# A graph network in one kernel: one row tile in five of the attention weights is transposed by a DMA on 16-bit halves instead of by TensorE

## What is computed

```python
def _sparse_attention(x, src, dst, wq, bq, wk, bk, wv, bv, wo, bo):
    q = (x @ wq + bq).reshape(N, H, Dh) * Dh ** (-0.5)
    k = (x @ wk + bk).reshape(N, H, Dh)
    v = (x @ wv + bv).reshape(N, H, Dh)
    scores = jnp.einsum('ehd,ehd->eh', q[src], k[dst])
    ex = jnp.exp(scores - smax[src])
    attn = ex / denom[src]
    out = jax.ops.segment_sum(attn[:, :, None] * v[dst], src, num_segments=N)
    return out.reshape(N, D) @ wo + bo
```

## Time and profile before

| | |
|---|---|
| time, median of 3 runs | 1119.53 us (1119.40 to 1120.54) |
| span of the profiled execution | 1117.2 us (its time outside the profile isn't recorded) |
| PE busy | 1066.1 us, 95% of the span |
| DVE busy | 773.4 us, 69% |
| ACT busy | 577.6 us, 52% |
| POOL busy | 673.3 us, 60% |
| granted TensorE clock, mean | 0.992 of full speed |
| one turn of the middle loop | 141.1 us |

### The profile page before, as it was taken

One profiled execution on the slowest core, in us unless ns is written; L12 is line 12 of the kernel. 1 busy time (PEld: TensorE's weight loads), 2 busy tenths in 40 slices (PEclk: granted clock), 3 DMA queues, 4 the chain that ended last, 5 costly groups with the idle time before them and its releaser, 6 DMA issues.

```text
span 1117.2 us, 20722 instructions
## 1 busy us (share of the span) xinstructions
PE 1066.1 (95%) x6808; PEld 987.7 (88%) x6808; DVE 773.4 (69%) x1535; ACT 577.6 (52%) x1032; POOL 673.3 (60%) x923
## 2 busy tenths in 40 slices
...
DMA packets 40963, 56.92 MB, mean 51 GB/s; under 512 B 14312, under 2 KB 14812, under 8 KB 40735
## 3 DMA queue, kind: packets, MB, share of 16 engines
...
q10 hardware_dynamic: 260, 0.21, 0.1%
...
## 4 chain that ended last, share of the span: by engine, by line
PE 79%; DVE 6%; POOL 5%; ACT 4%; issue 3%; DMA 2%; DVEq 0%; POOLq 0%; SPq 0%; PEldq 0%; ACTq 0%
PE ps L340 42%; PE ps L1768 8%; PE ps L362 8%; PE ps L786 5%; PE ps L2101 3%; PE ps L2028 3%; PE ps L2402 3%; POOL w_lo L380 2%; ACT away L737 1%; PE ps L2065 1%; PE ps L1259 1%; PE ps L1246 1%; PE ps L1742 1%; DMA w_raw<-L_gnn_wk 1%; PE ps L1220 1%
## 5 line engine op out<-in xcount | busy, mean ns | idle before, releaser
L380 POOL TENSOR_TENSOR w_lo<-w_raw,w_hi 128x512 fp32r<-128x512 f32 x152 | 204.8, 1348 | 12.7
L340 PE MATMUL ps<-yt_hi,w_hi 128*128 128x314 f32 (+2 forms) x640 | 201.8, 315 | 2.8 <-DVE yt_lo L2236 1.6
L340 PE MATMUL ps<-yt_hi,w_lo 128*128 128x314 f32 (+2 forms) x640 | 197.6, 309 | 0.0
L340 PE MATMUL ps<-yt_lo,w_hi 128*128 128x314 f32 (+2 forms) x640 | 197.3, 308 | 0.0
L459 POOL TENSOR_SCALAR prob<-prob,rinv 125x628 f32<-125x628 f32 x160 | 126.4, 792 | 105.2 <-DVE rinv L444 86.9
L403 ACT ACTIVATE pt_hi<-ps 125x625 fp32r<-125x625 f32 x160 | 109.2, 694 | 102.9 <-PE ps L362 101.7
L377 POOL TENSOR_SCALAR w_hi<-w_raw 128x512 fp32r<-128x512 f32 x152 | 97.7, 643 | 95.3 <-DMA w_raw<-L_gnn_wo 28.8
L340 PEld LDWEIGHTS ps<-yt_hi,w_hi 128*128 128x128 f32 x640 | 121.8, 190 | 5.9 <-issue 4.4
L340 PEld LDWEIGHTS ps<-yt_hi,w_lo 128*128 128x128 f32 x640 | 121.7, 190 | 0.0
L340 PEld LDWEIGHTS ps<-yt_lo,w_hi 128*128 128x128 f32 x640 | 121.5, 190 | 0.1
L786 PE MATMUL ps<-oh_s,oh_d 125*125 125x314 bf16 x800 | 111.4, 301 | 10.1 <-DVE oh_s L639 6.8
...
## 6 DMA issues: line engine op xcount, KB each, us to landing
w_raw<-L_gnn_m_w SPq DMA_DIRECT2D x8, 1024.0 KB, 5.4
w_raw<-L_gnn_W SPq DMA_DIRECT2D x6, 1024.0 KB, 5.4
w_raw<-L_gnn_wv SPq DMA_DIRECT2D x4, 1024.0 KB, 6.1
w_raw<-L_gnn_wq SPq DMA_DIRECT2D x4, 1024.0 KB, 5.4
w_raw<-L_gnn_wk SPq DMA_DIRECT2D x4, 1024.0 KB, 7.4
w_raw<-L_gnn_wo SPq DMA_DIRECT2D x4, 1024.0 KB, 6.4
w_raw<-L_gnn_Wv SPq DMA_DIRECT2D x2, 1024.0 KB, 5.5
w_raw<-L_gnn_Wq SPq DMA_DIRECT2D x2, 1024.0 KB, 5.6
```

Of the source, the lines that this page charges most:

```text
L340: ins = pe.matmul(out_ap, lhs(i, kk), rhs(j, kk), start=kk == 0 and n == 0, stop=kk == count - 1 and n == 2)
L380: pool.tensor_tensor(w[slot][1][:, kk, 0:cols], w_raw[slot][:, kk, 0:cols], w[slot][0][:, kk, 0:cols].bitcast(FP32), ALU.subtract).then_in ...
```

## The change

Tile t0 of each of the four heads is no longer transposed by PE. In its place:

1. `ex:t{h}_0` on ACT (`act_planes`) copies the scaled 125x625 fp32 rows, seen as 125x1250 halfwords (U16), into one of two buffers `planes`: first the five blocks of the low halves, then the five of the high ones, each block in a 128x128 square.
2. `turn:t{h}_0` on SP is one `dma_start_transpose` of 128x10x128 halfwords (320 KB) from `planes` to `turned`. `turned` lies in the ring `prob`, in the place that the tile itself has (place 0). The ring's places are therefore 640 words wide, 628 before.
3. `jn:t{h}_0` on ACT (`act_joined`) waits for the DMA and puts the halves together again as fp32 words, in the `planes` buffer.
4. `hi:t{h}_0` and `lo:t{h}_0` read those words from SBUF instead of PSUM. `hi` waits for `pv{h-1}.0`, which reads the tile of the head before, and `pv{h}` waits for `lo` on a semaphore of its own.
5. `sc:s{h+1}_0` on DVE, which writes place 0 of the ring, waits for `jn:t{h}_0`.

The tables are changed by hand; on PE the four names become "-", so every other name keeps its slot. `scale` stays, and `ex` waits for it. To make room, the biases bo and m_b2 share one place `rows[1]`: m_b2 is loaded in the block when bo has been added, bo of the next block when m_b2 has been added; the last stage's ln_b row is loaded later. POOL clears both `planes` buffers once ahead of the first block (`memset`). The stage behind gets the same code for turned tiles, but its tables name none.

The core of the diff:

```diff
 LOOP_PE = """
-q0.0 q0.1 k1.0 k0.0 k0.1 k1.1 q1.0 s0_0 s0_1 s0_2 - q1.1 s0_3 q2.0 s0_4 t0_0 s1_0 - t0_1 q2.1 s1_1 t0_2 - k2.0
+q0.0 q0.1 k1.0 k0.0 k0.1 k1.1 q1.0 s0_0 s0_1 s0_2 - q1.1 s0_3 q2.0 s0_4 - s1_0 - t0_1 q2.1 s1_1 t0_2 - k2.0 t0_3
...
 LOOP_DVE = """
-lo:k0 lo:q0 lo:k1 sc:s0_0 sc:s0_1 inv:s0_0 sc:s0_2 inv:s0_1 sc:s0_3 lo:q1 sc:s0_4 lo:t0_0 inv:s0_2 sc:s1_0
-lo:t0_1 inv:s0_3 sc:s1_1 inv:s0_4 lo:t0_2 inv:s1_0 lo:q2 sc:s1_2 lo:t0_3 lo:t0_4 sc:s1_3 inv:s1_1 lo:k2
+lo:k0 lo:q0 lo:k1 sc:s0_0 sc:s0_1 inv:s0_0 sc:s0_2 inv:s0_1 sc:s0_3 lo:q1 sc:s0_4 inv:s0_2 sc:s1_0 lo:t0_1
+lo:t0_0 inv:s0_3 sc:s1_1 inv:s0_4 lo:t0_2 inv:s1_0 lo:q2 sc:s1_2 lo:t0_3 lo:t0_4 sc:s1_3 inv:s1_1 lo:k2 inv:s1_2
+sc:s1_4 sc:s2_0 inv:s1_3 lo:pv0 lo:t1_1 sc:s2_1 inv:s1_4 lo:q3 lo:t1_2 lo:t1_0 inv:s2_0 inv:s2_1 lo:k3 sc:s2_2
+lo:t1_3 sc:s2_3 lo:t1_4 inv:s2_2 inv:s2_3 sc:s2_4 lo:t2_1 inv:s2_4 lo:pv1 sc:s3_0 lo:t2_2 sc:s3_1 lo:t2_3
+lo:t2_0 sc:s3_2 inv:s3_0 sc:s3_3 inv:s3_1 lo:t2_4 inv:s3_2 sc:s3_4 inv:s3_3 inv:s3_4 lo:t3_1 lo:t3_0 lo:t3_2
...
 LOOP_ACT = """
-hi:q0 hi:k0 hi:k1 exp:s0_0 exp:s0_1 exp:s0_2 hi:q1 exp:s0_3 hi:t0_0 hi:t0_1 exp:s0_4 exp:s1_0 hi:t0_2 hi:q2
-exp:s1_1 hi:t0_3 hi:t0_4 exp:s1_2 hi:k2 hi:t1_0 exp:s1_3 hi:pv0 exp:s1_4 exp:s2_0 hi:t1_1 exp:s2_1 hi:q3
+hi:q0 hi:k0 hi:k1 exp:s0_0 exp:s0_1 ex:t0_0 exp:s0_2 hi:q1 exp:s0_3 hi:t0_1 exp:s0_4 jn:t0_0 hi:t0_0 exp:s1_0
+hi:t0_2 hi:q2 exp:s1_1 hi:t0_3 hi:t0_4 exp:s1_2 ex:t1_0 hi:k2 exp:s1_3 hi:pv0 exp:s1_4 jn:t1_0 exp:s2_0 hi:t1_1
+hi:t1_0 exp:s2_1 hi:q3 hi:t1_2 hi:k3 hi:t1_3 ex:t2_0 exp:s2_2 hi:t1_4 exp:s2_3 hi:t2_1 exp:s2_4 jn:t2_0 hi:pv1
+hi:t2_2 hi:t2_0 hi:t2_3 exp:s3_0 exp:s3_1 ex:t3_0 hi:t2_4 exp:s3_2 exp:s3_3 hi:t3_1 exp:s3_4 jn:t3_0 hi:t3_0
...
+LOOP_SP = """
+turn:t0_0 turn:t1_0 row:1 load:q load:k turn:t2_0 turn:t3_0
+""".split()
...
+    def act_planes(act, u, buf):
+
+        halfwords = prob[:, u % RING_P, 0:N].bitcast(U16).rearrange("p (a b e) -> p e a b", a=TILES, e=2)
+        act.activation(planes[buf][0:R, :, 0:R].rearrange("p (e a) b -> p e a b", e=2), halfwords,
+                       ACT.Copy).then_inc(s_planes, 1)
+
+    def act_joined(act, u, buf, turned_count):
+
+        act.wait_ge(s_turned, turned_count)
+        halfwords = joined[buf][:, 0:N].bitcast(U16).rearrange("p (a b e) -> p e a b", a=TILES, e=2)
+        act.activation(halfwords, turned[u % RING_P][0:R, :, 0:R].rearrange("p (e a) b -> p e a b", e=2),
+                       ACT.Copy).then_inc(s_joined, 1)
...
+                    sp.dma_start_transpose(turned[unit_of(name) % RING_P][:], planes[n % 2][:]).then_inc(s_turned, 16)
...
                 if kind == "sc":
                     u = int(name[1]) * TILES + t
+                    before = f"t{int(name[1]) - 1}_{t}"
+                    if before in middle_turned:
+                        dve.wait_ge(s_joined, it * TURNS + middle_turned.index(before) + 1)
...
+                if kind == "ex":
+                    u, n = unit_of(name), middle_turned.index(name)
+                    act.wait_ge(s_sc, it * UNITS + u + 1)
```

More of the change, by code:

```diff
@@ L143 @@
-p4.1 a1_1 v0 n1_3 a1_2 v1 n1_4 a1_3 v2 a1_4 v3 v4
+q0.0 q0.1 k1.0 k0.0 k0.1 k1.1 q1.0 s0_0 s0_1 s0_2 - q1.1 s0_3 q2.0 s0_4 - s1_0 - t0_1 q2.1 s1_1 t0_2 - k2.0 t0_3
+s1_2 t0_4 - k2.1 s1_3 pv0.0 - s1_4 pv0.1 s2_0 - t1_1 s2_1 q3.0 t1_2 q3.1 k3.0 k3.1 s2_2 t1_3 t1_4 s2_3 pv1.0
+s2_4 - t2_1 - pv1.1 s3_0 t2_2 s3_1 t2_3 s3_2 s3_3 t2_4 s3_4 pv2.0 - t3_1 pv2.1 t3_2 - t3_3 t3_4 pv3.0 pv3.1 o0.0
+n2_0 o0.1 - o1.0 o1.1 o2.0 n2_1 o2.1 a2_0 o3.0 o3.1 n2_2 n2_3 a2_1 a2_2 o4.0 o4.1 n2_4 a2_3 f1.0 f2.0 a2_4 f0.0
@@ L144 @@
+f1.1 f0.1 f2.1 f3.0 f3.1 p0.0 n1_0 p1.0 p0.1 p1.1 p2.0 p2.1 p3.0 p3.1 a1_0 n1_1 p4.0 n1_2 p4.1 a1_1 v0 n1_3 a1_2
+v1 n1_4 a1_3 v2 a1_4 v3 v4
 """.split()
 LOOP_DVE = """
-lo:k0 lo:q0 lo:k1 sc:s0_0 sc:s0_1 inv:s0_0 sc:s0_2 inv:s0_1 sc:s0_3 lo:q1 sc:s0_4 lo:t0_0 inv:s0_2 sc:s1_0
-lo:t0_1 inv:s0_3 sc:s1_1 inv:s0_4 lo:t0_2 inv:s1_0 lo:q2 sc:s1_2 lo:t0_3 lo:t0_4 sc:s1_3 inv:s1_1 lo:k2
-lo:t1_0 inv:s1_2 sc:s1_4 sc:s2_0 inv:s1_3 lo:pv0 lo:t1_1 sc:s2_1 inv:s1_4 lo:q3 lo:t1_2 inv:s2_0 inv:s2_1
-lo:k3 sc:s2_2 lo:t1_3 sc:s2_3 lo:t1_4 inv:s2_2 inv:s2_3 sc:s2_4 lo:t2_1 lo:t2_0 inv:s2_4 lo:pv1 sc:s3_0
@@ L150 @@
[L150 to L154, removed]
```

195 lines of the change are left out of this document (137 added, 58 removed).

## The result

The changed kernel takes **1156.93 us** (median of 4 runs, 1156.46 to 1157.7) for 1119.79 of the kernel before in the same comparison: 1.0335 times as long, interval 1.0322 to 1.0348. Slower by 37.1 us, or 9.3 us in each of four turns. The profiled execution took 1156.46 us, its span 1154.7.

The account below looks back on a forecast made before the run. TensorE was taken as the bound, with 0.6 us idle in 63. Shifts reaching +6.6 us at pv3.0, plus 0.5 for head 2, made 7.1 a turn; four turns, +28.4 on 1119.5, gave 1148 us, range 1131 to 1173.

Parts of the forecast that it names:

- The gain: TensorE, each t0 tile: dropping five transposes saves 0.54 us, 8.7 us over sixteen tiles, an upper bound.
- L: Transposing transfer of 320 KB, from `ex` done to landed: taken as 5.4 us, between 3.4 and 8.4.
- rival (1): Transposing DMA: the transfer is quick, near 3.4 us, giving 1139 us; chance 0.20.
- ScalarE's copies: `ex` and `jn` on ScalarE: 1.23 us each, advancing the engine by about 1.12 us.
- The signal behind `jn`: From `jn`'s end on ScalarE at 386.72 to sc:s1_0's start on VectorE at 386.77.
- Head 0: sc:s1_0 waits for `jn:t0_0`, lo:t0_2 frees its PSUM slot later, so TensorE starts s1_2 2.0 us later.
- Head 1: `jn:t1_0` delays sc:s2_0, whose slot q3 needs: q3 starts 1.4 us later.
- Head 2: `jn:t2_0` has a window of 4.9 us; a transfer of 5.4 us passes on 0.5 us.
- Head 3: `ex:t3_0` idles for the scale: shift of 4.6 us at exp:s3_4, 6.6 us at pv3.0.
- The clock: TensorE in the changed profile: granted clock expected at 1.00.
- Rival (3): TensorE's clock falls behind head 3's waits of 1.9 and 2.5 us, 2 us more a turn: 1156; chance 0.10.
- Signs: Expected in the changed profile: turn at 148 us for 141.1, 37 us of new TensorE waits in four attention parts.

Follow-up runs that it names:

- two_tuned: Kernel before with only t1_0 and t2_0 turned by DMA, steps placed where ScalarE idles, lo:k2 ahead of inv:s1_1 on VectorE: 1115.87 us, ratio 0.9968.
- no_transfer: Changed kernel without the 16 transposing DMAs and `jn`'s waits for them; `jn` reads constant zeros: 1161.89 us, ratio 1.0345 to the kernel before.
- heads_1_2: Changed kernel with only t1_0 and t2_0 turned by DMA, t0_0 and t3_0 back on TensorE: 1134.81 us, ratio 1.0129 to the kernel before.
- copy_only: Kernel before plus one ScalarE copy of 1250 halfwords behind exp:s0_4, for which sc:s1_0 waits; no DMA: 1127.99 us, ratio 1.0078.

## Why the prediction was right, and where it was wrong

The direction, the mechanism (joins on ScalarE hold up scores on VectorE, and these hold slots that TensorE wants) and the range held. 1148 was 9 us short, and it is luck that it was no more: that distance hides errors of both signs.

- **The gain, 0.54 us a tile:** in two_tuned 0.80 us a turn arrive of the two tiles' 1.08; where the other 0.28 goes the rows don't show, for TensorE waits no longer there than before. In the change the gain is swallowed, as forecast.
- **L, the transfer, taken as 5.4 us: wrong.** It lands 3.4 us after its issue begins, my lower bound, and no `jn` of the change waits for it; no_transfer agrees. That is rival (1)'s case. Counted as L was, from the end of `ex`, it was 3.7 us in two_tuned, where a `jn` does wait for it (392.61 + 1.24 to 397.57). Only in heads_1_2, behind the loads of m_w, was it 5.3, near my 5.4. The Trainium skill, "Advanced Engine Details and Errata", section X-Bar Transpose (TRN2), has transposing DMAs as fast as regular ones, and the trace agrees: 3.4 us for 320 KB lies where plain loads would, between 2.9 for 156 KB and 5.4 for 1024 KB. The Trainium skill's 1309 ns for one square, "VectorE: DVE Perf Modes", The three transpose paths, does not add up in series: ten squares would be an estimated 13 us. My forecast owes the transfer 2.2 us a turn that did not come; with L = 3.4 my own sum was 4.9 a turn, 1139, for the measured 9.3. The other terms missed 4.4 a turn.
- **ScalarE's copies:** `ex` 1.245 us for my 1.23, `jn` 1.62. I had named strided halfwords as the risk and priced the two alike. `jn` takes 1.66 from start to start for 1.12: half a microsecond on the path in each of heads 0, 1 and 3.
- **The signal behind `jn`:** 395.01 + 1.63 to 396.91 is 0.27 us; I had written 0.05 (386.72 to 386.77).
- **Head 0, forecast +2.0:** sc:s1_0 was 2.9 late for my 2.1 (the longer `jn`, the signal), lo:t0_2 3.0 for my 2.4, and with the clock's fall sc:s1_2 3.6. copy_only, where lo:t0_0 stays ahead of the score, pays 2.0 to 2.1 at the full clock. t0_2 itself waited for s1_0's slot, where I had followed only the slot of lo:t0_2. **Head 1, +1.4:** it was 2.0, and `jn` explains 0.5 of the 0.6. **Head 2, 0.5 for the transfer:** not there.
- **Head 3, 4.6 up to exp:s3_4:** it was 7.3, of it 3.6 in place of 2.0 brought along from head 0. ex:t3_0 idles 2.54 us for the scale, as said. Behind it I left an instruction out: `lo:t3_0` stands ahead of `lo:t3_2` in VectorE's order, and took 1.66 us instead of 0.8. From exp:s3_4 to pv3 the shift grew by 2.0, for my 0.3 at L = 3.4 (4.6 to 4.9). That it matches the 2.0 of my forecast (4.6 to 6.6 at L = 5.4) is luck: no `jn` waited for the transfer.
- **The clock:** "granted clock at 1.00" was wrong. Rival (3), at 0.10, came true in kind: four falls, 6.9 us, but none behind head 3's waits, where I had looked; two stand behind head 0's t0_2 and two behind q3.0, which waits for head 1's join. Its 1156 us is within a microsecond of the measured time by luck, since it holds the 2.2 us a turn of a transfer that cost nothing.
- **Signs:** the turns took 151.3, 150.2, 150.2 and 149.9 us for my 148 (from TensorE's first matmul of one, at 220.06, 371.36, 521.55, 671.79, to that of the next, the last to 821.72); new waits of TensorE were 30 us by its rows (32.7 less 2.4 before) for my 37, and about 0.5 us behind each that the rows don't show.

The sum over the four turns is thus: falls 6.9, waits 30 by the rows, some 9 for what lies behind them, less 8.7 for the transposes: 37. The 9 is the difference left over and was not measured by itself; copy_only shows it for one wait (0.48), and five a turn would make an estimated 9.6.

What stays open: why t0_2's wait let the clock fall in two turns of the change (1.58 and 1.57 us) and not in the other two (1.57 and 1.61), nor in copy_only (1.60). Falls moved with every edit, and in no_transfer the mean clock differed from run to run of one kernel. Nor was the 1.66 us of lo:t3_0 taken apart; GpSimd's w_lo ran beside it, from 448.11 for 1.27 us.
